# Multiplying the routing weight ahead of the gate, and splitting the gated product out of PSUM, in a four-layer attention/MoE/RWKV kernel

## The reference

```python
x = x + attn_a(_layernorm(x), W_Q, W_K, W_V)          # causal attention, one head of 128
x = x + ffn(_layernorm(x), Wg, W1, W2, W3, Ws1, Ws2, Ws3)
x = x + attn_b(_layernorm(x), ...)                    # RWKV time mix (a scan over tokens) and channel mix
x = x + ffn(_layernorm(x), Wg, W1, W2, W3, Ws1, Ws2, Ws3)

def swiglu(x, w1, w2, w3):
    return silu(x @ w1) * (x @ w3) @ w2
def ffn(x, ...):                                      # 32 experts of hidden size 64, one shared of 128
    scores = softmax(x @ Wg); weights, indices = top_k(scores, 4)
    for e in range(32):                               # at most C tokens for each expert, in token order
        y = y.at[tok].add(swiglu(x[tok], W1[e], W2[e], W3[e]) * w[:, None])
    return y + swiglu(x, Ws1, Ws2, Ws3)
```

## Time and profile before

| | us |
|---|---|
| median of 3 runs | 976.08 |
| the runs | 970.86, 977.25, 976.08 |
| span of the profiled execution | 975.2 |
| the profiled execution beside its span | no other time is shown for it; the span lies inside the range of the runs |
| instructions | 14773 |

### The profile page before, as it was taken

One profiled execution on the slowest core, in us unless ns is written; L12 is line 12 of the kernel. 1 busy time (PEld: TensorE's weight loads), 2 busy tenths in 40 slices (PEclk: granted clock), 3 DMA queues, 4 the chain that ended last, 5 costly groups with the idle time before them and its releaser, 6 DMA issues. The chain is left out here.

```text
span 975.2 us, 14773 instructions
## 1 busy us (share of the span) xinstructions
PE 826.6 (85%) x3938; PEld 642.9 (66%) x3938; DVE 807.1 (83%) x1637; ACT 570.4 (58%) x1066; POOL 657.5 (67%) x487
## 2 busy tenths in 40 slices
PE   3479999898999977879879788798797887999997
PEld 2358777677777756657657576575575665778775
DVE  4557777676868889999999999999999999976765
ACT  2246565565656654665766647566576475486654
POOL 5417676776777876776776857767668576676665
PEclk8689999999999998989989999999898998999999
DMA  8033423324151512314304131144142311434353
GB/s 267 0 89 88 89 73 73 74 70 104 46 129 46 130 44 60 74 43 90 87 18 115 44 89 44 44 89 97 29 103 54 89 52 45 107 80 104 86 131 74
DMA packets 45326, 77.32 MB, mean 79 GB/s; under 512 B 3040, under 2 KB 11360, under 8 KB 44896
## 3 DMA queue, kind: packets, MB, share of 16 engines
q1 hardware_dynamic: 44992, 76.57, 33.0%
q10 hardware_dynamic: 288, 0.20, 0.1%
HBM read 73.62 MB, written 3.15 MB: 79 GB/s over the span
## 5 line engine op out<-in xcount | busy, mean ns | idle before, releaser
L400 POOL TENSOR_TENSOR m_h<-m_v,m_wb 128x512 f32<-128x512 f32 x256 | 358.8, 1406 | 214.9 <-DVE m_v L1016 153.8
L508 ACT ACTIVATE m_th<-pa 128x512 f32<-128x512 f32 x232 | 137.9, 595 | 169.2 <-PE pa L723 139.0
L293 DVE TENSOR_TENSOR m_hl<-m_h,m_hh 128x512 fp32r<-128x512 f32 x174 | 177.2, 1019 | 65.4 <-ACT m_hh L646 64.6
L646 ACT ACTIVATE m_hh<-m_h 128x512 fp32r<-128x512 f32 x272 | 170.8, 628 | 65.6 <-POOL m_h L400 61.5
L721 PE MATMUL pa<-m_xh,w1h 128*128 128x512 f32 (+1 forms) x272 | 131.4, 483 | 46.9 <-DVE m_v L1028 46.9
L1016 DVE TENSOR_TENSOR m_v<-m_th,pb 128x512 f32<-128x512 f32 x216 | 145.4, 677 | 16.6 <-ACT m_th L508 9.1
L293 POOL TENSOR_TENSOR m_hl<-m_h,m_hh 128x512 fp32r<-128x512 f32 x98 | 131.6, 1342 | 27.5 <-ACT m_hh L646 27.3
L721 PE MATMUL pb<-m_xh,w3h 128*128 128x512 f32 (+1 forms) x272 | 114.1, 419 | 16.5 <-DVE m_v L1016 15.7
L733 PE MATMUL py<-m_hh,w2h 128*128 128x512 f32 x272 | 109.6, 403 | 3.6 <-POOL m_hl L293 3.6
L723 PE MATMUL pa<-m_xh,w1l 128*128 128x512 f32 (+1 forms) x272 | 109.9, 404 | 0.0
L722 PE MATMUL pa<-m_xl,w1h 128*128 128x512 f32 (+1 forms) x272 | 109.8, 404 | 0.0
(11 more groups left out here) (209 smaller groups left out, 1621.4 us busy)
## 6 DMA issues: line engine op xcount, KB each, us to landing
m_wb<-w_scratch SPq DMA_DIRECT2D x126, 512.0 KB, 6.4
x_sb<-in_x SPq DMA_DIRECT2D x8, 256.0 KB, 7.8
m_wb<-in_w SPq DMA_DIRECT2D x2, 1024.0 KB, 7.1
x_out<-x_sb SPq DMA_DIRECT2D x8, 256.0 KB, 6.9
f_kk<-in_w SPq DMA_DIRECT2D x1, 1024.0 KB, 9.8
w_scratch<-r_wT SPq DMA_DIRECT2D x16, 64.0 KB, 1.6
m_wb<-w_scratch SPq DMA_DIRECT2D x8, 128.0 KB, 3.0
mt<-in_mats SPq DMA_DIRECT2D x1, 768.0 KB, 11.1
```

Of the source, the lines that this page charges most:

```text
L293: eng.tensor_tensor(m_hl[:, at, :], m_h[:, HIDDEN_AT[p], :], m_hh[:, at, :].bitcast(F32), ALU.subtract)\
L400: pool.tensor_tensor(m_h[:, HIDDEN_AT[p], :], gated(p), m_wb[:, p % (GRING * GP), :], ALU.mult).then_inc(sig["m_h"], 1)
L508: ins = act.activation(m_th[:, p % 2, :], pa[p % 2][:, :], ACT.Silu)
L646: act.activation(m_hh[:, SPLIT_AT[p], :], m_h[:, HIDDEN_AT[p], :], ACT.Copy).then_inc(sig["m_hh"], 1)
```

## The change

The routing weight is moved ahead of the gate. POOL forms `m_tw` = `m_th`·`m_wb`, with the same instruction as before but on silu(a) in place of the gated product. DVE multiplies `pb` by `m_tw` in place, in PSUM. ACT rounds `m_hh` from the PSUM bank, and DVE takes `m_hl` from the bank too: all 17 low parts of an iteration are now DVE's, and so is the low part of the routed input (`m_xl`), since POOL does not reach PSUM. PE may start `pb` of unit k only when `m_hl` of unit k-2 is there. `m_v` and `m_h` are gone. The splits follow one slot behind the unit (`SPLIT_LAG` 1), the product with W2 three slots behind (`LAG` 3), and PE does it between `pa` and `pb`. Later iterations have two tanh units (10 and 11). A number of steps of the other layers move by a slot, and all loops are written out.

```diff
-LAG = 4
-SPLIT_LAG = 2
-LOW_ON_POOL = (
-    (0, 4, 6, 7, 8, 9, 11, 12, 14, 15),
-    (6, 9, 12, 15),
-    (2, 9, 14),
-)
-TANH_UNITS = {False: tuple(range(9, 14)), True: (10,)}
+LAG = 3
+SPLIT_LAG = 1
+TANH_UNITS = {False: tuple(range(9, 14)), True: (10, 11)}
...
# GpSimd, unit
-                pool.wait_ge(sig["m_v"], done(UNITS * g + p + 1))
-                wait_split(pool, *unit_before(g, p, since_last_use(HIDDEN_AT, p)))
-                pool.tensor_tensor(m_h[:, HIDDEN_AT[p], :], gated(p), m_wb[:, p % (GRING * GP), :],
-                                   ALU.mult).then_inc(sig["m_h"], 1)
+                if by_tanh(g, p):
+                    pool.wait_ge(sig["m_u"], tanh_units(g, p) + 1)
+                else:
+                    pool.wait_ge(sig["m_th"], k + 1)
+                wait(pool, "m_h", UNITS * g + p - 1 if p >= 2 else UNITS * (g - 1) + PAIRS - 1 + p)
+                pool.tensor_tensor(m_tw[:, p % 2, :], m_th[:, k % 2, :], m_wb[:, p % (GRING * GP), :],
+                                   ALU.mult).then_inc(sig["m_tw"], 1)
...
# ScalarE, split_high
-                act.activation(m_hh[:, SPLIT_AT[p], :], m_h[:, HIDDEN_AT[p], :], ACT.Copy).then_inc(sig["m_hh"], 1)
+                act.wait_ge(sig["m_h"], k + 1)
+                wait(act, "m_y", k + 1 - SPLITS)
+                act.activation(m_hh[:, k % SPLITS, :], pb[k % 2][:, :], ACT.Copy).then_inc(sig["m_hh"], 1)
...
# TensorE, unit
-                wait(pe, "m_v", done(k + 1 - lag))
-                up(pb[p % 2], w3h, w3l, g, p).then_inc(sig["m_b"], 1)
+                out_step(g, p)
+                wait(pe, "m_hl", k - 1)
+                up(pb[k % 2], w3h, w3l, g, p).then_inc(sig["m_b"], 1)
...
# VectorE, unit and split_low
+                tw = m_tw[:, p % 2, :]
+                dve.wait_ge(sig["m_tw"], PAIRS * g + p + 1)
+                dve.wait_ge(sig["m_b"], k + 1)
...
+                    dve.tensor_tensor(gated, tw, gated, ALU.mult).then_inc(sig["m_h"], 1)
...
+                dve.wait_ge(sig["m_hh"], k + 1)
+                dve.tensor_tensor(m_hl[:, at, :], pb[k % 2][:, :], m_hh[:, at, :].bitcast(F32),
+                                  ALU.subtract).then_inc(sig["m_hl"], 1)
...
# VectorE: a_xn of attention from slot 1 to 2; GpSimd: its a_rs from slot 0 to 1
-                if slot == 1:
+                if slot == 2:
                     dve.wait_ge(sig["a_rstd"], n + 1)
                     normalise(a_xn, chunk(n), a_mv, a_rs, "a_xn")
...
# ScalarE, time_step: the two exps from slot 10 to 11, t_k from 8 to 9, t_v from 9 to 10
-                if slot == 10:
+                if slot == 11:
                     act.wait_ge(sig["t_a0"], m + 1)
...
-            with act.Fori(1, B - 3) as g:
+            for g in range(1, B - 3):
```

More of the change, by code:

```diff
@@ L60 @@
 N_MATS = 12
-def since_last_use(places, p):
-    return next(n for n in range(1, len(places) + 1) if places[(p - n) % len(places)] == places[p])
 def hybrid_kernel(nc, x_in, att_mats, mats, key_in, vecs, w_gate, w1_in, w3_in, w2_in, x_out):
@@ L146, in hybrid_kernel @@
         m_th = sb("m_th", [P, 2, S])
-        m_v = sb("m_v", [P, 2, S])
-        m_h = sb("m_h", [P, 3, S])
-        m_hh = sb("m_hh", [P, 4, S], F32R)
-        m_hl = sb("m_hl", [P, 4, S], F32R)
+        m_tw = sb("m_tw", [P, 2, S])
+        m_hh = sb("m_hh", [P, SPLITS, S], F32R)
+        m_hl = sb("m_hl", [P, SPLITS, S], F32R)
         m_y = sb("m_y", [P, S])
@@ L320, in _ @@
                 sp.dma_start(chunk(c), xv[c]).then_inc(sig["in_xr"], 16)
-            for name in ("m_v", "m_h", "m_y", "m_x"):
-                sp.sem_inc(sig[name], BASE)
             def spread_weights(q):
@@ L482, in _ @@
             iteration(B, tmix=3, cmix=2, pro=B + 1)
-            with pool.Fori(B + 1, 2 * B - 3) as g:
+            for g in range(B + 1, 2 * B - 3):
                 iteration(g, tmix=g - (B - 3), cmix=g - (B - 2), pro=g + 1)
@@ L942, in _ @@
             iteration(0, att=2, pro=1)
-            with pe.Fori(1, B - 3) as g:
+            for g in range(1, B - 3):
                 iteration(g, att=g + 2, pro=g + 1)
@@ L948, in _ @@
             iteration(B, tmix=3, cmix=2, pro=B + 1)
-            with pe.Fori(B + 1, 2 * B - 3) as g:
+            for g in range(B + 1, 2 * B - 3):
                 iteration(g, tmix=g - (B - 3), cmix=g - (B - 2), pro=g + 1)
@@ L1017, in unit @@
                     return
-                tanh = TANH_UNITS[late]
-                through, before = ("m_u_late", LATE) if late else ("m_u", 0)
-                count = len(tanh) * (g - before) + tanh.index(p) + 1
-                dve.scalar_tensor_tensor(out=m_th[:, r, :], in0=m_th[:, r, :], scalar=1.0, in1=pa[r][:, :],
-                                         op0=ALU.add, op1=ALU.mult).then_inc(sig[through], 1)
-                low()
-                dve.wait_ge(sig["m_b"], k + 1)
-                dve.wait_ge(sig[through], count)
@@ L1299, in _ @@
             iteration(0, att=2, pro=1)
-            with dve.Fori(1, B - 3) as g:
+            for g in range(1, B - 3):
                 iteration(g, att=g + 2, pro=g + 1)
```

317 lines of the change are left out of this document (138 added, 179 removed).

## The result

The changed kernel takes 1074.73 us (median of 4 runs, 1073.66 to 1075.56), the kernel before 976.07 beside it: a ratio of 1.101, interval 1.097 to 1.105. It is 98 us slower; I had forecast 31.

A forecast was written before the change was run, and what follows sets the result against it. PE was taken to bound the early iterations and the tail, DVE iterations 5 to 12, more than half the time. 975.2 + 12 (late) + 20 (early) + 3 (tail) - 3 (loops) = 1007 us, range 968 to 1036.

The forecast's parts named there:

- The stages and their bounds: Iterations 0 to 4 PE-bound at 51.7 us each, 5 to 12 DVE-bound at 64.4, 13 to 15 PE-bound.
- DVE's own work and POOL's holds: Iterations 5 to 12: DVE's work -1.5 us an iteration, fewer holds by POOL -4.6 (bounds 0 and 8).
- DVE's waits in the late stage: Iterations 5 to 12: waits of 8.2 us an iteration against 0.8 before, +7.4.
- what the shorter lag adds: Late stage: DVE's split one slot behind the gate waits for ACT's `m_hh`, queueing later DVE work; +7.4 us an iteration.
- Early stage: Iterations with PE as bound: `a_xn` comes later for PE; +4 us each for five, +20 (0 to +35).
- The tail: Iteration 14: late weights now hold the gate and `pb` of unit 2; +3 us (0 to +6).
- Loops: Written-out loops save 0.37 us in each of eight looped iterations: -3 us (-3 to 0).
- PE's reordering: PE's product with W2 moved, same nine matmuls: costs nothing by itself.
- POOL near 530 us: Sign in the profile after: POOL's busy time near 530 us.
- The slow one: Chain bounds everywhere, 1050 us: in-place PSUM write 0.1 us dearer (27), early stage loses 7 us an iteration; chance 0.10.
- The faster one: DVE's stage shrinks, freed from POOL's holds: 955 us, if `m_hh` waits stay under 3 us an iteration; chance 0.17.
- The one at 976: Buffers swallow the waits: late -3, early +1 us an iteration, up to 20 us of waits on top; chance 0.17.

The follow-up runs named there:

- lag 2 and the new placement: Changed kernel with side steps as changed, gated product in SBUF, splits two slots later, W2 product four, gate not waiting for POOL's product: 1056.1 us.
- lag 1 and the old one: Changed kernel with side steps in the slots of before, product in PSUM, splits one slot later, gate not waiting for POOL's product: 990.0 us.
- the old placement: Side steps in the slots of the kernel before on every engine, single late tanh unit; otherwise as the changed kernel, two POOL steps later: 1115.7 us.
- the lag alone: Changed kernel with gated product in SBUF: splits one slot later 1112.3 us, two slots later (W2 product four) 1114.3 us.
- the unrolled kernel: Kernel before with its loops written out on every engine, nothing else changed: 971.6 us, ratio 0.995.
- without the gate's wait: Changed kernel, but DVE's gate takes silu(a) without waiting for POOL's product, which nobody reads: 1029.4 us, ratio 1.053.
- earlier weights: Changed kernel with each iteration's routing weights taken from the copy of the iteration before: 1069.4 us, ratio 1.096.
- POOL's short product: Changed kernel with POOL's product by the routing weight cut to 64 of 512 columns, every wait kept: 966.6 us, ratio 0.990.
- the same cut: Kernel before with loops written out and POOL's product cut to 64 of 512 columns: 875.9 us, ratio 0.897.

## Why the prediction was wrong

The direction was right and the size a third. Point by point:

- **The stages and their bounds**: right. The late stage decided the matter.
- **DVE's own work and POOL's holds, -6.1 us an iteration** (-1.5 and -4.6): measured -4.2 (495.7 to 462.0 us over eight). The costs of the single instructions were right: 684 ns a split, 688 an in-place product, no spread, and `t_qq` and `t_eb` went from 1.69 and 1.76 us to 0.75 each. What I left out is that the holds move with POOL's steps: `t_d1`, 0.68 us before, now takes 1.50 and the sum behind it 1.63. The Trainium skill, SBUF — State Buffer, section Who interferes with whom, has a DVE instruction with two SBUF inputs contend with GpSimd, and one with at most one not. The trace agrees in both directions: 684 ns from PSUM against 898 from SBUF for the same split.
- **DVE's waits in the late stage, +7.4 us an iteration**: this is the step that failed. DVE's idle time rose by 12.3, from 2.7 to 15.0. Of the 8.2 that I had for the change, 6.1 were waits for `m_hh`; measured were 8.8. Those that I followed were right: 2.6 us at the split of unit 11 (2.7 forecast), 1.4 at unit 5 (1.4), 0.7 at unit 1 (0.8, for slots without side steps). But I counted ACT's queue alone, and took for granted that PE's `pa` is there when ACT comes to the silu. At units 8 and 15 it is not, and these two cost 3.7 us an iteration, where I had 1.2 for units 4, 7, 8 and 12 together and nothing for 15. The gate's waits for `m_tw` came to 2.9 us, where I had 0.8 for unit 10 alone. That one was right (0.79); the second tanh unit has the same wait again (0.82), and other units have the rest. `t_k` cost 0.7 (1.3 forecast). Waits for `r_mx` and `pb`, and gaps too short for the list of waits, add about 1.4. With the smaller relief that gives -4.2 + 12.3 = 8.1 us an iteration, 65 in all, where my sum had 1.3 and I took 1.5.
- **Its heading, "what the shorter lag adds", named the wrong cause.** With lag 2 and the new placement the wait for `m_hh` is 66 us; with lag 1 and the old one 29. The waits at units 8, 11 and 15 come with the placement. The short lag and the product in place, taken together in the old placement, leave the late stage as long as it was; the lag alone was tried in the new placement only, where it changed nothing clear.
- **Early stage, +4 us an iteration**: measured +6.5 (203.2 to 229.0 over four), or 7.7 against the unrolled kernel. That the gate's dependence on POOL does it is shown: without the wait 204.7. The way that I described is not: PE waited for `a_xn` 1.6 us in the whole stage, less than the 8.0 before, and 18.4 us for `m_hl` ahead of `pb`. And a term is missing: PE's matmuls themselves took 12 us longer, at a granted clock of 0.95 in place of 0.98; without the gate's wait the clock is 1.00 there and PE busy 190.7 us.

```profile
PE pb L650 <- DVE m_hl L953: 18.4, 13, 3.4
...
PE pu L628 <- DVE a_xn L919: 1.6, 2, 1.2
```

- **The tail, +3 us**: it came to +7. The late weights are a part of it, for earlier weights give 6 us back; 4.6 of the 7 stand as longer busy time of PE (118.4 us against 113.8).
- **Loops, -3 us**: -5 in all, but my price of 0.37 us came from the late stage, and there the gain was nothing; the early stage has it.
- **PE's reordering, nothing**: no run undoes it alone, so it is not shown either way. PE now waits 34 us for `r_carry`, a result of the routing, ahead of `pa`, but that comes with the slots of two routing steps; undoing that pair gave 5 us more in the median, with intervals that overlap.
- **POOL near 530 us**: it was 473; the 98 splits took 132 us with them, and its product takes 1328 ns in place of 1406.
- **The rivals.** The slow one, 1050, was nearest in time, with two reasons: the in-place write at 100 ns more is false, it is 11; the 7 us an iteration in the early stage came. The faster one was to be decided by DVE's waits for `m_hh` under 3 us an iteration; they were 8.8. The one at 976 had the late stage 3 us an iteration shorter, and it is 8 longer. (Its sum gives 956, and 976 only with all of the waits that it adds.) My range failed first in the late stage, whose +65 us lie beyond the +40 that I had as its upper bound. But with 40 there and the other stages as measured the time would still be 1050: the range ended at 1036, though its terms' upper ends add up to 1056, because I took them for unlikely together, and they came together.

The whole: 972 us unrolled; splits from PSUM with the short lag, `m_xl` with DVE and two POOL steps later, the gate still free, 990; the gate made to wait for POOL in that placement, 1116; the steps re-placed to lessen this, 1075. The placement gives 41 us back while the gate waits, and costs 39 while it doesn't. So its cost belongs to the weight ahead of the gate too: that is what makes it necessary. This last sentence is argued from the four numbers; a placement that I didn't try might do better, and which of the moved steps cost, or how much the second tanh unit does, no run separates.

Not tried: DVE's split without its wait for ACT, with a wrong result, which would show in one number what the late waits are worth. Not settled: how much PE's lower clock adds. In the late stage the granted clock is 0.90 after and 0.95 before, and PE's 2040 matmuls take 470 us in place of 433; in the early stage, where PE is the bound, the 12 us of longer matmuls count in full. One place in the late stage, PE behind its wait for `r_carry`: its first row, and the windows of that stretch and of one 4 us later.

```profile
620.68 1.01 PE L781 MATMUL pq<-ident,r_w 128*32 128x128 f32 x4 [4.86 <-DVE r_carry L1097]
...
620.68:623.00 2.32, 2.32 (x8) 1.83 (x9) 2.29 (x4) 0.00 (x0) 0.00 (x0) 0.50 0.00 0
624.70:626.00 1.30, 1.30 (x7) 0.95 (x6) 1.30 (x2) 1.30 (x3) 0.27 (x1) 1.00 0.00 0
```

After 4.9 us without a matmul PE runs at 1.2 GHz (0.50), its matmuls of 512 columns at 0.63 to 0.77 us; at 2.4 GHz (1.00) they take 0.39. The stretch around the split of unit 8 above, at 0.53, is of the same kind, so that wait of DVE holds some of the clock's cost; how much is not shown. The clock isn't the main cause in this stage: with POOL's short product the changed kernel has 0.95 in it and is still 63 us longer than the kernel before with the same cut, which has 0.97.

The fastest kernel that computes everything is the one before with its loops written out, 971.6 us, half a per cent under the kernel before.

## What to carry to other kernels

When a product moves from behind a step to ahead of it, the engine that makes it turns from one that may trail into one that must lead, for every unit; ask first what else stands in its queue and whom that waits for, since its side steps now stand in front of everybody. Price such a move together with the placement that it forces. A wait for an engine is a wait for all that this engine waits for: follow each one back past the first queue, here from DVE to ACT to PE. When a wait has been priced, test its cause crosswise (each lag with each placement) before naming it. A cut that gives back all of a loss proves nothing until the same cut has been made in the kernel before: here it gave 108 us, and it gave the kernel before 96.
